# An RWKV block with an fp4 feed-forward on one core: VectorE adds the normalised input to the first of five mixed inputs in place of GpSimd, under new hand-written stage orders

## The reference

```python
def _time_mix(x, p):
    sx = _shift(x) - x
    xxx = x + sx * p['x_maa']
    mix = jnp.tanh(xxx @ p['tm_w1']).reshape(b * t, 5, E)
    mix = jnp.einsum('nfe,fed->fnd', mix, p['tm_w2'])...
    mw, mk, mv, mr, mg = mix
    wx = x + sx * (p['w_maa'] + mw)      # the first of the five mixed inputs
    kx = x + sx * (p['k_maa'] + mk)      # and likewise vx, rx, gx
    ...
    w = jnp.tanh(wx @ p['td_w1']) @ p['td_w2']
    w = jnp.exp(-jnp.exp(p['time_decay'] + w))
    out = _wkv(r, k, v, w, p['time_first'])   # recurrence over time
    ...                                       # group norm, gate g, @ p['Wo']

def _forward(x, params):
    for i in range(L):
        x = x + _time_mix(_ln(x, p['ln1_w']), p)
        x = x + _channel_mix(_ln(x, p['ln2_w']), p)
    return _ln(x, params['ln_out_w'])
```

## Time and profile before

| what | value |
|---|---|
| median of 3 runs | 2931.07 us (2931.01 to 2931.13) |
| profiled execution, its own time | 2933.48 us |
| span of the profiled execution | 2931.7 us |
| PE busy | 2725.0 us, 93% |
| DVE busy | 2349.0 us, 80% |
| ACT busy | 1389.7 us, 47% |
| POOL busy | 1279.2 us, 44% |

### The profile page before, as it was taken

The page is one execution under the profiler, slowest core; times in us unless marked ns, Lnnn a source line. Parts: engine busy times, 40 slices in busy tenths (PEclk is TensorE's granted clock), DMA queues, the critical chain, the costliest instruction groups (busy, mean ns, idle before and its releaser), DMA issues.

```text
span 2931.7 us, 82824 instructions
## 1 busy us (share of the span) xinstructions
PE 2725.0 (93%) x34621; PEld 2171.8 (74%) x34621; DVE 2349.0 (80%) x5345; ACT 1389.7 (47%) x2899; POOL 1279.2 (44%) x1457
## 2 busy tenths in 40 slices
...
DMA packets 36849, 41.77 MB, mean 14 GB/s; under 512 B 3272, under 2 KB 35200, under 8 KB 36480
## 3 DMA queue, kind: packets, MB, share of 16 engines
...
q10 hardware_dynamic: 784, 0.16, 0.1%
...
## 4 chain that ended last, share of the span: by engine, by line
PE 74%; ACT 13%; DVE 7%; issue 4%; POOL 1%; ACTq 0%; DMA 0%; DVEq 0%; POOLq 0%
PE ps_all L1530 12%; PE ps_all L1317 11%; PE ps_all L1516 10%; PE ps_all L1549 8%; PE ps_all L1325 8%; PE ps_all L1567 5%; PE ps_all L1428 3%; PE ps_all L1355 3%; ACT L898 3%; PE ps_all L1309 2%; PE ps_all L1341 2%; ACT tok L898 2%; PE ps_all L1423 2%; PE ps_all L1486 2%; PE ps_all L1497 1%
## 5 line engine op out<-in xcount | busy, mean ns | idle before, releaser
L771 POOL TENSOR_TENSOR mixin<-mixin,hT_tm 128x512 f32<-128x512 f32 x320 | 398.0, 1260 | 384.9 <-DVE mixin L1118 384.1
L1516 PE MATMUL ps_all<-chan,cwk 128*128 128x256 f32 x1536 | 374.0, 391 | 6.2 <-DVE chan L1097 5.5
L1530 PE MATMUL ps_all<-cwv,chan 128*128 128x256 f32 x1536 | 348.4, 383 | 0.6 <-DVE S L1194 0.6
L1516 PEld LDWEIGHTS ps_all<-chan,cwk 128*128 128x128 f32 x1536 | 288.6, 193 | 58.2 <-issue 17.2
L1530 PEld LDWEIGHTS ps_all<-cwv,chan 128*128 128x128 f32 x1536 | 286.7, 190 | 49.6 <-issue 10.3
L1118 DVE SCALAR_TENSOR_TENSOR mixin<-ps_all,vcol,sxrk 128x256 f32<-128x256 f32 x640 | 271.5, 473 | 29.9 <-PE ps_all L1355 19.8
L912 ACT ACTIVATE chan<-ps_all 128x512 f32<-128x512 f32 x192 | 114.9, 598 | 265.9 <-PE ps_all L1516 265.9
L751 POOL TENSOR_TENSOR rstd<-var,powc 128x2 f32<-128x2 f32 x224 | 178.2, 796 | 123.6 <-DVE var L1057 120.2
L1168 DVE COPY_PREDICATED att<-masks,ps_all 128x256 f32<-128x256 uint8 x384 | 203.3, 530 | 11.5 <-DVE att L1168 0.5
L1549 PE MATMUL ps_all<-gateT,ffn_work 128*128 128x352 f32 x512 | 184.1, 483 | 5.0 <-ACT ffn_work L871 2.6
L795 POOL TENSOR_TENSOR grstd<-gvar,powc 128x8 f32<-128x8 f32 x64 | 115.6, 1807 | 150.2 <-DVE gvar L1201 150.2
...
## 6 DMA issues: line engine op xcount, KB each, us to landing
...
```

The source lines that it names most:

```text
L771: pool.tensor_tensor(m, m, hT["tm", l][:, :, :, 1:P + 1].rearrange("p k c t -> p (k c) t"), ALU.add).then_inc(ev["mixed"][b], 1)
L1516: ins = pe.matmul(bank(b, "ck", lj, "k")[:, m * TT:(m + 1) * TT], cwk[:, l, k, n:n + P], k_in[:, k, :], start=(k == 0), stop=(k == KC - 1))
L1530: ins = pe.matmul(bank(b, "cv", l, "v")[:, c * D:(c + 1) * D], relu[t // 2][:, t % 2, c * P:(c + 1) * P], cwv[:, l, t, :], start=(t == 0), ...
```

## The change

In the kernel, DVE's mf stage for f = 0 waits for its own two instructions and then does the addition itself. It increments an event of its own, "mixed_w", for which pw1 now waits; the counts of "mixed" and "mixed_w" are kept apart. POOL's lists no longer hold mf.0, neither for stream 0 nor for stream 1. The other additions stay on POOL.

```diff
-    "carried": (["turn"], 1), "shifted": (["mix", "cmix"], 1), "xxx": (["mix"], 1), "tanh": (["mix"], 1), "mixed": (["mf"], 1),
+    "carried": (["turn"], 1), "shifted": (["mix", "cmix"], 1), "xxx": (["mix"], 1), "tanh": (["mix"], 1), "mixed": (["mf"], 1), "mixed_w": (["mf"], 1),
...
-                if kind in kinds:
+                if kind in kinds and (name not in ("mixed", "mixed_w") or (arg[1] == 0) == (name == "mixed_w")):
...
                 ins.then_inc(free_of(b, *(("pw2", l, "w") if f == 4 else ("mf", lf, "m"))), 1)
+                if f == 0:
+                    emptied(v, i, b, "mf", lf, "m")
+                    m = mixes(b, f).rearrange("p k (c t) -> p (k c) t", t=P)
+                    v.tensor_tensor(m, m, hT["tm", l][:, :, :, 1:P + 1].rearrange("p k c t -> p (k c) t"), ALU.add).then_inc(ev["mixed_w"][b], 1)
...
-                after(pe, i, "mixed", b, "mf", (l, 0))
+                after(pe, i, "mixed_w", b, "mf", (l, 0))
```

ORDER, HEAD and TAIL are written anew for all four engines. The stages in them are the same but for POOL's mf.0; the tables start at another point of the cycle, and a part of the stages stands at other places. The table of POOL's steady cycle, shortened:

```diff
-    POOL: """0/1 lna.tm mix; 1/3 st.1; 4/4 lna.ffn; 1/3 gnb; 0/1 mf.0 mf.1 mf.3; 1/3 yt; 2/2 cv; 0/1 mf.2; 1/2 lna.tm; 3/3 lna.cm;
...
+        1/2 gnb; 0/0 mf.1 mf.3; 1/2 yt; 2/1 cv; 0/0 mf.2; 1/1 lna.tm; 3/2 lna.cm; 1/1 mix; 3/2 cmix; 0/0 mf.4 tot; 1/1 mf.1
```

More of the change, by code:

```diff
@@ L26 @@
 ORDER = {
[L27 to L38, removed]
@@ new lines @@
+    DVE: """0/1 sc.3 cp.2 cq.2 rs.3 cp.3; 1/2 mf.4 sc.1; 0/1 cq.3; 4/4 gu.1.0; 0/1 st.0 st.1; 1/2 rs.1; 0/1 gna; 1/2 sc.2; 4/4
+        gu.1.1; 0/1 gnb; 1/2 cp.0; 4/4 qa.1; 1/2 cp.1; 4/4 qc.1; 1/2 cq.1; 3/3 cv; 0/1 wo; 2/1 lna.cm; 1/2 pg; 2/1 lnb.cm; 1/2
+        rs.2 sc.3 cp.2; 0/0 lna.in lnb.in; 2/1 cmix; 0/0 h0; 4/4 dn; 1/2 cq.2; 4/3 lna.out; 0/0 lna.tm; 1/2 rs.3 cp.3; 0/0
+        lnb.tm; 4/3 lnb.out x2; 1/2 cq.3; 4/3 lna.ffn; 0/0 mix; 1/2 st.0; 4/3 lnb.ffn hf; 1/2 st.1 gna; 0/0 mf.0 mf.1 mf.3;
+        1/2 gnb; 4/3 qa.x qc.x; 2/1 cv; 0/0 mf.2; 1/2 wo; 1/1 lna.tm; 3/2 lna.cm; 1/1 lnb.tm; 3/2 lnb.cm; 4/3 gu.0.0; 0/0 mf.4
+        sc.1; 1/1 mix; 4/3 gu.0.1; 3/2 cmix; 0/0 rs.1; 1/1 mf.0 mf.1; 0/0 sc.2; 1/1 mf.3; 0/0 cp.0; 4/3 qa.0; 0/0 cp.1; 1/1
+        mf.2; 0/0 cq.1 pg; 4/3 qc.0; 0/0 rs.2""",
@@ new lines @@
+    AC: """0/1 sc.3; 4/4 ht.0; 1/2 sc.1; 4/4 gu.1.0; 0/1 kt gna; 3/3 ck.2; 4/4 gu.1.1; 3/3 cr; 1/2 pv sc.2; 0/1 yt; 4/4 qa.1; 1/2
+        pg; 4/4 ht.1; 2/1 turn.cm; 1/2 sc.3; 2/1 ck.0 ck.1; 0/0 turn.tm; 1/2 kt; 2/1 ck.2 cr; 0/0 mix; 1/2 gna yt; 0/0 pw1;
+        4/3 qa.x; 0/0 pk pr; 4/3 xt; 0/0 pw2; 4/3 gu.0.0; 1/1 turn.tm; 3/2 turn.cm; 0/0 sc.1; 4/3 gu.0.1; 0/0 pv; 1/1 mix; 3/2
+        ck.0; 0/0 sc.2; 1/1 pw1; 0/0 pg; 1/1 pk; 4/3 qa.0; 1/1 pr pw2; 3/2 ck.1""",
+    POOL: """0/1 gnb yt; 1/2 st.0; 3/3 cv; 2/1 lna.cm cmix; 0/0 lna.in; 4/4 dn; 4/3 lna.out; 0/0 lna.tm mix; 1/2 st.1; 4/3 lna.ffn;
+        1/2 gnb; 0/0 mf.1 mf.3; 1/2 yt; 2/1 cv; 0/0 mf.2; 1/1 lna.tm; 3/2 lna.cm; 1/1 mix; 3/2 cmix; 0/0 mf.4 tot; 1/1 mf.1
+        mf.3 mf.2 mf.4; 0/0 st.0; 1/1 tot; 0/0 st.1""",
```

283 lines of the change are left out of this document (140 added, 143 removed).

## The result

Nine executions of the changed kernel took 2940.49 us in the median (2934.44 to 2946.45), against 2931.13 (2927.72 to 2933.31) for nine of the kernel before. The ratio is 1.0033, with a 95% interval of 1.0023 to 1.0043: slower by a third of a per cent, some 9 us. Another set, timed later, gave 1.0026 (1.0015 to 1.0037). I had forecast 2928.5, 2.5 us less than before and no change that can be told; what came is 9 us more, clear of noise. The time lies inside the range of 2913 to 2942 only because the range was drawn to take in the slower rival; that is luck, not a forecast that held.

A forecast was written before the change was run, and what follows sets the result against it. TensorE, busy 97.5% of the steady part, was taken as the bound. Steady +1, head -3.5 and rest 0 made -2.5 us, 2931.0 for the profiled execution; against the other runs' median 2931.07 the forecast was 2928.5 us, range 2913 to 2942.

The forecast's parts named there:

- the slower rival: Steady part: layer 1's add delays the mask copy freeing lev.2's banks, +0.4 us a tile or more; 2939 us, chance 0.18.
- the step on layer 1's addition: Steady part: cq.1 0.75 us later, slack absorbs it, lev.3 starts as now; net 0 to +0.1 us a tile.
- The wait forecast at lev.2: Steady part, PE: a new wait of 0.3 to 0.5 us a tile for DVE's mask copy, replacing ht.0's.
- st.0 on POOL: Steady part: st.0 moves a few places in POOL's list, in front of no listed PE wait; nothing.
- DVE and POOL block one another: Layer 0: the new DVE add is held while POOL's grstd runs; +0.2 us a tile, 2934 us, chance 0.06.
- The head's term: Head, 0 to 133.5 us: reordered norm and grid stages bring wr of tile 1 3.5 us earlier; bounds +3.1 and -7.
- The tail: End of the kernel: lists rewritten with the same stages, no single wait removed; 0, bounds -3 and +3 us.
- the steady term: 26 steady tiles: layer 1's add nearly absorbed, layer 0's add and other moves nothing; +1 us, between 0 and +5.

The follow-up runs named there:

- order_only: The change with all w additions left on POOL (mf.0 back ahead of mf.1): 2941.29 us, ratio 1.0021 to the kernel before, steady tile 84.75 us.
- add_only: The lists of the kernel before, with the w addition on VectorE for both layers: 2946.77 us, ratio 1.0043, steady tile 85.01 us.
- ck1_first: The change with TensorE's ck.1 ahead of pw2 and lev.2 again, as before: 2941.66 us, ratio 1.0030 to the kernel before, steady tile 84.91 us.
- st0_back: The change with POOL's st.0 of stream 1 behind cv of stream 3 again: 2937.13 us, ratio 1.0014 to the kernel before, steady tile 84.75 us.
- after_again: The change itself, unaltered, timed and profiled a second time: 2943.45 us, ratio 1.0026 to the kernel before.
- tail_new: The kernel before with the change's lists from tile 29's first transposes on, all additions on POOL: 2938.49 us, ratio 1.0010.
- order_st0: The change with all additions on POOL and st.0 of stream 1 behind cv again: 2933.25 us, ratio 0.9998 to the kernel before, tile 84.57 us.
- head_new: The kernel before with the change's lists up to tile 5's first transposes, w addition on POOL: 2932.97 us, ratio 0.9993.
- cycle_on: The change with its steady cycle carried on through tiles 29 and 30, its end lists only from there: 2940.46 us, ratio 1.0028 to the kernel before.

## Why the prediction was wrong

Two steps of the steady part failed, and one of the tail.

**The rows of before were read for one chain only.** The first is the step on layer 1's addition: "lev.3 comes at 1426.2 to 1426.3, as now". I followed the 0.75 us shift to cq.1 and lev.2 and stopped there, because ScalarE's chain set lev.3. The same VectorE list goes on to cq.2, which lev.3 needs as well. In the trace of before it ends at 1425.78, 0.42 us ahead of lev.3 at 1426.20:

```profile
1424.76 1.02 DVE L1168 COPY_PREDICATED att<-masks,ps_all 128x256 f32<-128x256 uint8 x2
```

and VectorE stands still nowhere between 1411.74 and there. In the change the addition is the second of these:

```profile
1405.56 0.88 DVE L1116 SCALAR_TENSOR_TENSOR mixin<-ps_all,vcol,sxrk 128x256 f32<-128x256 f32 x2 [0.19 <-PE ps_all L1357]
1406.47 0.69 DVE L1122 TENSOR_TENSOR mixin<-mixin,hT_tm 128x512 f32<-128x512 f32 x1
...
1419.04 1.01 DVE L1170 COPY_PREDICATED att<-masks,ps_all 128x256 f32<-128x256 uint8 x2
```

It took 0.69 us, and with the end of its overlap shifts its follower by 0.73 (1407.08 - 1405.56 = 1.52, where the follower came 0.79 later): 0.75 was right for the follower. It doesn't all arrive at cq.2. From the start of mf.0 to the end of cq.2 it was 14.04 us (1411.74 to 1425.78) and is 14.49, so 0.45 more; some 0.16 comes back at the quantising's L586 (0.35 us long beside POOL's L771 in before, 0.19 in the change), and 0.11 where the first scaling starts closer behind L609. PE starts lev.3 0.14 us after cq.2 ends (1420.05 to 1420.19), so of the 0.42 some 0.28 was slack, and 0.45 less 0.28 leaves 0.17. order_only against the change shows 0.15: there 14.19 became 14.49, because the second scaling is 1.11 us long while POOL does the w addition and 0.68 when it doesn't. add_only shows 0.39 in the old order, where ht.0 feels it. The term was 0 to +0.1 a tile and measured +0.15. The wait forecast at lev.2, 0.3 to 0.5 us, is 0.17, and ck1_first shows that it isn't what costs.

**st.0 on POOL was priced at nothing,** with the reason that it stands in front of no wait of the earlier trace rows. It doesn't, but it slows VectorE beside it, and that stands in front of the transposes' wait: +0.15 a tile, shown by st0_back. It shows in POOL's own time too: 1221.8 us where I had about 1200, with the 128 L788 at a mean of 796 ns (633 before). A rival named this mechanism ("DVE and POOL block one another", 0.06), but at the addition itself, beside grstd, where it did not happen: the addition's group of 64 has a mean of 692 ns. The Trainium skill ("SBUF — State Buffer", "Who interferes with whom") says that a VectorE instruction with two SBUF inputs contends with a GpSimd instruction that reads SBUF. By that rule, the trace agrees, in both directions: L604 takes 1.19 for 0.89 beside st.0, and st.0 (L788) 1.26 for 0.62 beside L602.

**The head's term was right**, in its mechanism and nearly in its size. wo of tile 0 was to be 3.1 us later, the first channel mix 2.6 earlier, wr of tile 1 3.5 earlier. In the timeline of PE of after_again:

```profile
89.28 3.75 PE L1530 MATMUL ps_all<-wo,mixin 128*128 128x256 f32 x8 [3.44 <-POOL mixin L1001]
...
102.65 3.75 PE L1721 MATMUL ps_all<-chan,cwk 128*128 128x256 f32 x8 [3.29 <-DVE chan L1298]
...
125.76 1.89 PE L1522 MATMUL ps_all<-mixin,wr 128*128 128x256 f32 x8
```

85.64 became 89.28 (+3.6), 105.57 became 102.65 (-2.9), 130.65 became 125.76 (-4.9). By tile 4 3.0 us of gain are left, at the same clock of 0.72 as before; in the first profiled execution 8.2, at 0.77.

**The tail was priced at 0 with bounds -3 and +3,** with no working but that no single wait was seen to go. Its three full tiles lose 5.6 to 6.0, twice the bound. tail_new puts the whole tail at 0.0010, 2.9 us (0.3 to 5.6): at the bound.

**The sum.** Forecast +1 - 3.5 + 0. In place of it, by after_again's profile, +5.1 - 3.0 + 7.7, with 1.7 of the last at a lower clock than in before. By the timings of whole runs it is some 8 to 10 for the steady part (order_st0), -2 for the head (head_new, not clear of noise) and +2.9 for the tail (tail_new). By either, the steady term (+1, at most +5) was too small. The slower rival ("The layer-1 add is late at one place: lev.2's banks", 2939) had the time nearly right and the mechanism half: it is layer 1's addition and a POOL instruction, but neither acts through lev.2's banks (ck1_first), and the POOL instruction isn't the one it named.

Still open: why the three end tiles lose. cycle_on shows that their order does it, not which stage. Whether the end lists change the granted clock of the drain is open too. And the spans of two profiles of the change, +1.0 and +9.9 us over before, differ mostly by the clock of the head and the drain, so the single parts aren't known better than some 3 us each.
